# Six of eight units merged on TensorE, the scatter begun in the rank stage, preparation reordered, shorter stages by token

## The reference, cut to what matters

```python
x = x + conv(ln_c(x))                          # x: (4, 64, 64, 256), layer norm over channels
t = tokens(x)                                  # 16384 tokens of 256
t = t + ffn(ln_t(t), W_gat, att_src, att_dst, b_gat, ln_gamma, ln_beta, W1, b1, W2, b2, edge_index)

def conv(x):                                   # per image: 4096 tokens
    corr = einsum('bmf,bnf->bmn', x3, x3) / F
    s = -sort(-corr, axis=-1)                  # each row of 4096 sorted, descending
    return take(s, ranks, axis=-1)             # 256 ranks, evenly spaced from 1 to 4095

def ffn(x, ...):                               # a graph attention (1048576 edges) routes 4 experts
    h = x @ W_gat; e = leaky_relu(a_src[src] + a_dst[dst])
    ee = exp(e - segment_max(e, dst)[dst]); alpha = ee / segment_sum(ee, dst)[dst]
    scores = layernorm(segment_sum(h[src] * alpha, dst) + b_gat).mean(heads)
    w = softmax(top_2(scores))
    return sum over experts of gate * (gelu(x @ W1[e] + b1[e]) @ W2[e] + b2[e])
```

## Time and profile before

| | us |
|---|---|
| median of 3 runs | 30719.29 (30713.63 to 30737.62) |
| the profiled execution's own time | 30707.68 |
| its span | 30706.0 |

### The profile page before, as it was taken

One profiled execution on the slowest core, in us unless ns is written; L12 is line 12 of the kernel. 1 busy time (PEld: TensorE's weight loads), 2 busy tenths in 40 slices (PEclk: granted clock), 3 DMA queues, 4 the chain that ended last, 5 costly groups with the idle time before them and its releaser, 6 DMA issues. The chain is left out here.

```text
span 30706.0 us, 514061 instructions
## 1 busy us (share of the span) xinstructions
PE 26132.4 (85%) x182003; PEld 12435.8 (40%) x182004; DVE 27866.9 (91%) x31378; ACT 20334.5 (66%) x30319; POOL 19826.0 (65%) x9076
## 2 busy tenths in 40 slices
PE   3888889989999999999999999989999999982473
PEld 2555543333333333333333333333333333332473
DVE  6888858999999999999999999999999999996435
ACT  1777777767767767767776776767777777763720
POOL 0000007898888888888888888888888898402610
PEclk8999999999999999999999999999999999996655
DMA  2000000000000000000000000000000000000104
GB/s 93 2 2 2 2 19 4 7 7 7 7 7 7 12 7 7 7 7 7 7 12 7 7 7 7 7 6 7 13 7 7 7 6 7 7 5 13 15 11 136
DMA packets 651242, 393.57 MB, mean 13 GB/s; under 512 B 425132, under 2 KB 604336, under 8 KB 646448
## 3 DMA queue, kind: packets, MB, share of 16 engines
q1 hardware_dynamic: 338034, 311.42, 3.2%
q0 software_dynamic: 290304, 22.40, 1.1%
q10 hardware_dynamic: 20288, 25.70, 0.2%
HBM read 196.49 MB, written 162.34 MB: 12 GB/s over the span
## 5 line engine op out<-in xcount | busy, mean ns | idle before, releaser
L1584 POOL DMA_INDIRECT sorted_d<-word_s,place_s x8192 | 18974.3, 2316 | 2642.8 <-issue 2476.8
L1496 ACT ACTIVATE z<-psum 128x1024 f32<-128x1024 f32 x10089 | 10181.7, 1054 | 2004.0 <-PE psum L1223 1258.5
L1395 DVE TENSOR_TENSOR arena<-arena 128x1024 f32<-128x1024 f32 (+16 forms) x5760 | 10843.3, 1883 | 442.8 <-ACT arena L1492 397.0
L1396 DVE TENSOR_TENSOR arena<-arena 128x1024 f32<-128x1024 f32 (+16 forms) x5760 | 10837.1, 1881 | 0.0
L1223 PE MATMUL psum<-z,net 64*64 64x512 f32 x72504 | 9163.8, 601 | 140.3 <-ACT z L1496 111.2
L1496 ACT ACTIVATE cst<-psum 128x1024 f32<-128x1024 f32 x5015 | 5303.4, 1058 | 979.2 <-PE psum L1223 635.0
L1223 PE MATMUL psum<-cst,net 64*64 64x512 f32 x36040 | 4826.4, 602 | 77.9 <-ACT cst L1496 51.0
L1223 PEld LDWEIGHTS psum<-z,net 64*64 64x64 f32 x72504 | 2425.6, 131 | 5275.3 <-issue 5178.5
L1216 PE MATMUL psum<-rows,arena 128*128 128x256 f32 x8192 | 2017.6, 402 | 1629.4 <-ACT arena L1492 1597.1
L1578 POOL DMA_DIRECT2D word_s<-words_d x64 | 37.5, 586 | 4830.5 <-ACT cst L1496 4702.1
L1038 ACT ACTIVATE arena<-cst,arena 128x128 bf16<-128x128 f32 x8320 | 2632.8, 389 | 610.1 <-PE psum L966 513.4
(11 more groups left out here) (231 smaller groups left out, 23519.1 us busy)
## 6 DMA issues: line engine op xcount, KB each, us to landing
sorted_d<-word_s,place_s POOLq DMA_INDIRECT x8192
y_d<-ys SPq DMA_DIRECT2D x256, 256.0 KB
arena<-y_d SPq DMA_DIRECT2D x64, 1024.0 KB, 5.5
arena<-in_x SPq DMA_DIRECT2D x34, 512.0 KB, 5.1
x<-in_x SPq DMA_DIRECT2D x65, 256.0 KB
xnt_d<-arena SPq DMA_DIRECT2D x32, 512.0 KB, 3.1
hk_d<-arena SPq DMA_DIRECT2D x32, 512.0 KB, 4.3
arena<-hk_d SPq DMA_DIRECT2D x4, 4096.0 KB
```

The source lines that it names most:

```text
L1395: nc.vector.tensor_tensor(hi_out, hi_in, lo_in, ALU.max)
L1396: return nc.vector.tensor_tensor(lo_out, hi_in, lo_in, ALU.min)
L1496: last = nc.scalar.activation(flat, bank, ACT.Abs)
L1584: pool.indirect_dma_start(out=b.sorted_d[:, :], out_offset=bass.IndirectOffsetOnAxis(ap=place_s[:, s, j:j + 1], axis=0), in_=word_s[:, s, ...
```

## The change

- Six of the eight units are merged. VectorE's stages with p = 128 have 1024 keys per row, and TensorE has 272 ticks to a pair.
- The `carry` copies are ScalarE's, at fixed half ticks of the order (`CARRY_AT`: 2, 3, 19, 26, 78, 84, 142, 149, 214, 220 of 272). VectorE still waits for them (`carried`).
- In `prepare` the token part comes first, with statistics a step ahead, two buffers towards TensorE and ScalarE, and the next load issued before the stores. The edge part follows, and TensorE and ScalarE run the whole front end of pair 0 (`FIRST_PAIR`) between its groups of count matmuls. SP stores the words.
- In `rank` the places are turned to integers and stored super by super, and POOL scatters the first 14 supers. The other 50 follow in `pool_rows`, each group of 8 DMAs waiting for a count of VectorE's finished half stages. The one-hots lie elsewhere in the arena; their number and size are the same.
- In `segment_max` 4 of the 16 spreading operations are VectorE's.
- In `segment_sum` one-hots are bf16, values and look-up rows are split into three bf16 parts (24 and 60 columns instead of 8 and 20), the small operations are done once for four chunks, and the words are loaded a round ahead.

```diff
+EARLY_SUPERS = 14
+PACE = 8
...
-MERGED_UNITS = 4
+MERGED_UNITS = 6
...
+    ALONE = 10
...
             with sp.Fori(0, N_X) as i:
...
+                    k = i * 2 + s
+                    sp.wait_ge(normed, k + 1)
+                    nxt = ((k + 2) % (TILES // 4))
+                    sp.dma_start(xs[s], x_q[bass.ds(nxt, 1)].rearrange("o p q d -> (o p) q d")).then_inc(x_in[s], 16)
+
+                    sp.wait_ge(turned_copied, k + 1)
+                    tok = k * 512
                     sp.dma_start(b.xnt_d[:, :, bass.ds(tok, 512)], xt[s]).then_inc(xt_out[s], 16)
                     sp.dma_start(b.hk_d[:, :, bass.ds(tok, 512)], ht[s]).then_inc(xt_out[s], 16)
-
-                    nxt = ((i * 2 + s + 2) % (TILES // 4))
-                    sp.dma_start(xs[s], x_q[bass.ds(nxt, 1)].rearrange("o p q d -> (o p) q d")).then_inc(x_in[s], 16)
+            for s in range(2):
+                sp.wait_ge(xt_out[s], 32 * N_X)
+            sp.dma_start(b.xnt[:], b.hk_d[:, :, 0:M]).then_inc(b.hk_in, 16)
+            sp.dma_start(b.rows[:], b.xnt_d[:, :, 0:2 * P]).then_inc(b.rows_in, 16)
+            for k in range(2 * N_E):
+                sp.wait_ge(words_made, k + 1)
+                sp.dma_start(b.words_d[:, k * ECHUNK:(k + 1) * ECHUNK], words[:, k % 2, :]).then_inc(word_out[k % 2], 16)
+                if k + 2 < 2 * N_E:
+                    sp.wait_ge(edges_read, k + 1)
+                    load_edges(k + 2)
...
+            with dve.Fori(0, N_X) as i:
+                for s in range(2):
+                    k = i * 2 + s
+                    t = Tally(dve, dve_step, base=k * X_STEPS + (x_base + 2))
+                    statistics(t, 1 - s, i + (1 + s))
+                    dve.wait_ge(std_ready, k + 1)
+                    newton(nc, t, rstd, rtmp, var[:, s, :], std[:, s, :])
+
+                    dve.wait_ge(turned, i * 2)
+                    for q in range(4):
+                        last = nc.vector.tensor_scalar(xn[s][:, q, :], xs[s][:, q, :], mv[:, s, q, 0:1],
+                                                       rstd[:, q:q + 1], ALU.subtract, ALU.mult)
+                    last.then_inc(normed, 1)
...
-                    pe.wait_ge(turned_copied, k)
+                    pe.wait_ge(turned_copied, i * 2)
...
+            pe.wait_ge(turned_copied, 2 * N_X)
+            done = 0
+            for k in range(2 * N_E):
+
+                pe.wait_ge(edges_read, k)
+                for u in range(SUBS):
+                    pe.wait_ge(hot_ready, k * SUBS + u + 1)
+                    l16 = hot16[u % 2].rearrange("p j b -> p (j b)")
+                    l8 = hot8[u % 2].rearrange("p j b -> p (j b)")
+                    for g in range(8):
+                        last = nc.tensor.matmul(psum[:, 6, 0:64], l16[:, g * 128:g * 128 + 128],
+                                                l8[:, g * 64:g * 64 + 64], start=(u == 0 and g == 0),
+                                                stop=(u == SUBS - 1 and g == 7))
+                    last.then_inc(hot_used, 1)
+                    upto = max(k * SUBS + u + 1 - ALONE, 0) * len(FIRST_PAIR) // (2 * N_E * SUBS - ALONE)
+                    for s, n in FIRST_PAIR[done:upto]:
+                        front_matmuls(nc, b, pe, z, 0, s, n)
+                    done = upto
 
...
+                    deviation(1 - s, k + 2)
...
+            for s, n in FIRST_PAIR:
+                front_copy(nc, b, act, z, 0, s, n)
...
+                    dve.wait_ge(rank_used, (k + 1) * GROUPS)
+                    v = places[:, s, :]
+                    nc.vector.tensor_scalar(over[:, s, :], v, BIG, 2.0 * BIG, ALU.is_lt, ALU.mult).then_inc(over_made, 1)
+                    dve.wait_ge(over_made, k + 1)
+                    dve.wait_ge(place_out[s], i * 16)
+                    nc.vector.scalar_tensor_tensor(place_i[:, s, :], v, -BIG, over[:, s, :], ALU.add,
+                                                   ALU.add).then_inc(place_made, 1)
...
+            with sp.Fori(0, SUPERS // 2) as i:
+                for s in range(2):
+                    k = i * 2 + s
+                    sp.wait_ge(place_made, k + 1)
+                    sp.dma_start(b.place_d[:, bass.ds(k * SUPER, SUPER)], place_i[:, s, :]).then_inc(place_out[s], 16)
...
+            with pool.Fori(0, EARLY_SUPERS // 2) as i:
+                for s in range(2):
+                    pool.wait_ge(place_out[s], (i + 1) * 16)
+                    scatter(nc, b, pool, i, s)
+            for k in range(SCAT_SEMS):
+                pool.wait_ge(b.scattered[k], EARLY_SUPERS * SCAT // SCAT_SEMS * 16)
...
+def scatter(nc, b, pool, i, s, paced=False):
+
+    per_sem = SCAT // SCAT_SEMS
+    pool_in, scattered = b.pool_in, b.scattered
+    for k in range(SCAT_SEMS):
+        pool.wait_ge(scattered[k], i * (2 * per_sem * 16) + (s * per_sem * 16 if s else 0))
+    pool.sem_inc(b.settled[1], 1)
+    col = (i * 2 + s) * SCAT
+    pool.dma_start(b.word_s[:, s, :], b.words_d[:, bass.ds(col, SCAT)]).then_inc(pool_in[s], 16)
+    pool.dma_start(b.place_s[:, s, :], b.place_d[:, bass.ds(col, SCAT)]).then_inc(pool_in[s], 16)
+    pool.wait_ge(pool_in[s], (i + 1) * 32)
+    pool.sem_inc(b.settled[1], 1)
+    for j in range(SCAT):
+
+        if paced and j % PACE == 0:
+            pool.wait_ge(b.sorted_, ((i - EARLY_SUPERS // 2) * 2 + s) * 2 * N_FULL + (j * 2 * N_FULL // SCAT + 1))
+            pool.sem_inc(b.settled[1], 1)
+        pool.indirect_dma_start(
+            out=b.sorted_d[:, :], out_offset=bass.IndirectOffsetOnAxis(ap=b.place_s[:, s, j:j + 1], axis=0),
+            in_=b.word_s[:, s, j:j + 1], in_offset=None, bounds_check=CAPACITY - 1,
+            oob_is_err=False).then_inc(scattered[j % SCAT_SEMS], 16)
 
 
...
+    work = [(1 if s >= FIRST_MERGE else (M - LO) / M) if s < N_FULL else 0.5 for s in range(N_STAGES)]
+    CARRY_AT = {(p, which): round(H_BODY / BODY_PAIRS * sum(work[:first_of(p) + which + 1]) / sum(work))
+                for p in MERGES for which in range(2)}
...
-            def carry(source, target, to, p, which, i, s):
-
-                dve.wait_ge(sorted_, (i * N_FULL + (s + 1)) * 2)
-                nc.vector.tensor_copy(edges_of(target[:, 0:to], p, which),
-                                      edges_of(source[:, 0:to], p, which)).then_inc(carried, 1)
...
-                        for which in range(2):
-                            if h == 0 and k == p >> (which + 1):
-                                f = first_of(p)
-                                carry(keys[f % 2], keys[(f + 1) % 2], whole, p, which, i, f)
...
+            def carry(i, p, which):
+
+                s = first_of(p)
+                act.wait_ge(sorted_, (i * N_FULL + (s + 1)) * 2)
+                to = 2 * (M - LO) if s < FIRST_MERGE else 2 * M
+                nc.scalar.activation(edges_of(keys[(s + 1) % 2][:, 0:to], p, which),
+                                     edges_of(keys[s % 2][:, 0:to], p, which), ACT.Copy).then_inc(carried, 1)
+
+            def carries(i, place):
+                for (p, which), at in CARRY_AT.items():
+                    if place == at:
+                        carry(i, p, which)
 
...
+                        sorts = (body - back) * BODY_PAIRS + (r - 1)
+                        if not isinstance(body, int) or 0 <= sorts < PAIRS - 1:
+                            carries(sorts, place)
...
+            for place in range(H_BODY // BODY_PAIRS):
+                ffn_piece(PAIRS - 2, place)
+                carries(PAIRS - 1, place)
...
+            with pool.Fori(EARLY_SUPERS // 2, ECOLS // SCAT // 2) as i:
...
+                    scatter(nc, b, pool, i, s, paced=True)
...
+            def spread_share(i, s):
+
+                dve.wait_ge(got_in[s], (i + 1) * (16 * EQ))
+                dve.wait_ge(other_ready, i * N + (s + 1))
+                dve.sem_inc(b.settled[0], 1)
+                for h in range(HEADS):
+                    for q in DVE_Q:
+                        last = nc.vector.tensor_scalar(spread[s][:, h, q, :], other[s][:, q, :], MASKED,
+                                                       got[s][:, q, h:h + 1], ALU.mult, ALU.add)
+                last.then_inc(share_ready[s], 1)
...
+                for s in (0, 1):
+                    spread_share(i, s)
...
+                    if s + 2 < N:
+                        spread_share(i, s + 2)
...
-                        for q in range(EQ):
+                        for q in ACT_Q:
...
+                    pe.wait_ge(share_ready[s], i + 1)
...
+                sp.wait_ge(low_ready, i)
+                sp.dma_start(word.rearrange("p (s q) -> p s q", s=N), round_of(sorted_c, i)).then_inc(word_in, 16)
+                sp.wait_ge(value_ready, i)
+                sp.dma_start(got.rearrange("p (s q) f -> p s (q f)", s=N), round_of(gathered_c, i)).then_inc(got_in, 16)
...
+                dve.wait_ge(word_in, (i + 1) * 16)
+                nc.vector.tensor_scalar(low, word, 255, None, ALU.bitwise_and).then_inc(low_ready, 1)
```

(29 more changed lines are left out.)

492 lines of the change are left out of this document (235 added, 257 removed).

## The result

The changed kernel takes 37,704 us (median of 4 runs, 37,617 to 37,728), the kernel before 30,719 us (4 runs, 30,714 to 30,738). The ratio is 1.2267, 95% interval 1.2246 to 1.2289. I had forecast 29,947 us and at most 30,650.

A forecast was written before the change was run, and what follows sets the result against it. VectorE was taken to bound the sort, 27 us a pair ahead of TensorE, which would become the bound. 30706 + 52 + 260 - 618 (sort) - 100 - 367 = 29933, + 14 = 29,947 us; range 29,350 to 30,650.

The forecast's parts named there:

- Rank: Rank stage: +45 us for added VectorE operations and drains, +215 for the scatter beside it; +260 in the sum.
- what a DMA of POOL does to VectorE: Rank: each of 1792 scatter DMAs slows VectorE by 0.12 us, +215 us; bounds 0 and 450.
- Rival (b): Rank: POOL's scatter DMAs outlast the stage, at 2.62 us each 980 us more, whole 30,927 us; chance 0.12.
- My estimate from it, 6220 us for rank: Rank: by the skill's two-port lock a DMA takes 3.4 us, rank 6220 us, whole about 32,330 us.
- The carries: Sort: ScalarE's ten edge copies a pair add 4.7 us exposed; bounds 0, or all 11.5 and 3.4 more.
- Rival (c): Sort: edge copies fully exposed, VectorE and ScalarE waiting for each other, pair 370 to 372.5 us, whole 30,570 to 30,720; chance 0.15.
- TensorE's side (355.3): Sort: with two more merged units TensorE needs 355.3 us a pair and becomes the bound, 14 us above VectorE.
- VectorE's (341): Sort: VectorE's pair falls from 364.3 to 341 us, by 15.2 for halved stages and 8.1 for edge copies, +0.2.
- VectorE's lead over TensorE of 27 us: Sort, kernel before: VectorE leads TensorE by 27 us of 364 a pair; that margin decides the case.
- segment_max: segment_max: moving four of ScalarE's 16 spreading operations to VectorE saves 100 us; at most -230, at least +60.
- segment_sum: segment_sum: bf16 one-pass matmuls and fewer small operations cut a round to 12.2 us, -367 us; bounds -200 and -450.
- Prepare: Prepare: token part 224 us instead of 331, edge part 512, stage 761 us, +52; bounds -60 and +120.

The follow-up runs named there:

- e1: Changed kernel with no scatter in rank, all 64 supers scattered paced in the sort stage: 35,662 us, rank 3451 us.
- f2: Changed kernel without scatter in rank, carries on VectorE, POOL's pacing removed: 29,790 us, on a chip where the kernel before takes 30,436.
- f3: Changed kernel without scatter in rank or pacing, carries on VectorE, 24 register moves on POOL after each DMA: 29,808 us (kernel before 30,436).
- f4: Changed kernel, no rank scatter or pacing, carries on VectorE, 24 register moves per DMA, four merged units for six: 29,922 us (kernel before 30,436).
- h1: Changed kernel, no rank scatter or pacing, carries on VectorE, four merged units, segment_max spreading all on ScalarE: 31,142 us, ratio 1.0175 to kernel before.
- i1: Changed kernel, no rank scatter or pacing, carries on VectorE, four merged units, spreading on ScalarE, scatter begun after pair 1's front end: 30,623 us, ratio 0.9973.
- i2: Changed kernel, no rank scatter or pacing, carries on VectorE, six merged units, spreading on ScalarE, scatter begun after pair 1's front end: 37,684 us.
- f1: Changed kernel with no scatter in rank and carries on VectorE, pacing kept: 29,805 us, on a chip where the kernel before takes 30,436.
- g3: Changed kernel without scatter in rank, carries on VectorE, no pacing: 38,784 us, on a chip where the kernel before takes 30,734.
- sets 1 to 5: Five groups of follow-up runs, each on one chip beside the kernel before, which took 30,717, 30,436, 30,734, 30,718 and 30,707 us.

## Why the prediction was wrong, point by point

**Rank (+260 forecast, +2188 measured).** The step that failed is "what a DMA of POOL does to VectorE", priced at 0.12 us from the slowing of a small operation. In rank the one-hots take 286 to 289 ns beside the scatter against 280 without: 0.01 us. What the DMA does is make TensorE's and ScalarE's updates late, 1.31 us a DMA (e1). The work without the scatter is 157 us shorter than before, where I had added 45: VectorE's reduces wait 151 us, not 291. Rival (b) named the right stage and sign by the wrong way. POOL was never the bound: its DMAs ran every 1.28 us, half of the 2.50 us from which (b) decides, and ended at 3985, 2649 us before the stage did. By the Trainium skill, "SBUF — State Buffer", The "DVE blocks DMA" trap, an operation of VectorE in a two-port mode keeps GpSimd from writing a DMA's descriptors. My estimate from it, 6220 us for rank, is near the measured 5795, and still it does not explain them: here a DMA takes 974 ns, so the two-port lock does not show beside these one-hots. In the sort, beside rows of tensor_tensor, a DMA takes 1.83 us in the median (f2) and up to 146. It is held up there, though beside another operation than the copy that the trap names, and by less than the page's 3100 ns in the median. (My limit for POOL in rank, 2.07 us a DMA, comes to 2.11 by the terms that stand there; at 1.28 measured it changes nothing.)

**The carries (4.7 us a pair forecast, 27 measured: 388.7 less 361.5).** This is the second step that failed. I had both waits in hand (ScalarE at place 19, VectorE at place 214) and let the first cost nothing and the second "just fit". Such a wait, at a fixed place in a queue on which a second engine's pace depends, cost in both directions: 23 us on one side and 28 on the other. Rival (c) had the mechanism and, with 370 to 372.5, over half of the size.

**TensorE's side (355.3) and VectorE's (341).** VectorE's is right: three pairs of the changed kernel hold 1014.5 us of its work, 338 a pair. That TensorE sets the pair without the other two effects is right too, but at 361.5 to 362.4 us, 6 to 7 over the term, and no run tells where these come from. So the two units are worth 1.7 us a pair (f3 and f4) and not the 8.8 that lie between 364.1 and the term: TensorE and VectorE are now both full, and the merging has little left to give.

**What I did not see: the margin was doing a job.** I wrote that VectorE's lead over TensorE of 27 us decides the case. It does, the other way round: VectorE without a gap is what keeps POOL's DMAs 2.1 us apart. Take the lead away and every gap of VectorE lets POOL run at 1.28 us; that makes TensorE late, which makes VectorE's gap longer. h1's second window shows one such round, and i1 against i2 what it costs. Of the +4611 us of the sort, 1550 are the longer pair (24.6 x 63), 3440 the scatter beside 49 pairs (458.9 less 388.7), and -380 the two ends.

**A sign of it lay in the trace of before.** In segment_max 752 gathers are issued 1.30 us apart, and VectorE's reduce waited there for nobody, with 98 of TensorE's updates late by 1142 us in all, and none in f1: this row of the kernel before, and the same group in f1 on the other chip.

```profile
L1700 DVE TENSOR_REDUCE arena<-psum 128x4 f32<-128x2048 f32 x188 | 430.9, 2292 | 656.2 <-remote 608.7 <-issue 44.6 <-PE psum L1738 2.9
```

```profile
L1782 DVE TENSOR_REDUCE arena<-psum 128x4 f32<-128x2048 f32 x188 | 430.0, 2287 | 237.4 <-PE psum L1823 222.0 <-issue 14.9
```

**segment_max (-100 forecast, +155 measured).** Back on ScalarE alone the spreading gives 1280 us again (h1, i1), as before. So VectorE's share costs 150 us where updates are late: TensorE waits 614 us of the stage for it (L1791), for it stands in VectorE's queue behind reduces that wait for late updates. I had priced it at four operations of 0.25 us, exposed in a third of the chunks. Where they are not the stage takes 1029 us with the share; without it I have no run there.

**segment_sum (-367 forecast, -172 measured).** Outside my bounds. Two operations of successive rounds:

```profile
36811.71 2.50 DVE L1988 TENSOR_TENSOR arena<-cst,arena 128x512 bf16<-128x512 f32 x4
...
36827.74 2.50 DVE L1988 TENSOR_TENSOR arena<-cst,arena 128x512 bf16<-128x512 f32 x4
```

A round takes 16.0 us, not 12.2. TensorE's share fell even further than I said (212 / 47 = 4.5 us), but I had taken a round as the sum of TensorE's work and small change. It is one chain through three engines, in which TensorE, ScalarE and VectorE take turns; that batching the rounds' four chunks made it stricter I did not test.

**Prepare (+52 forecast, +125 measured).** Just outside my bound of +120. The edge part is as worked out, 517 us for 512. The token part is not: VectorE begins the one-hots at 321.4 us, not 249, so double buffering took 35 us off it and not 107. The step takes 9.2 us, not 7.0. What I left out of it is the load: in 31 of the 32 steps VectorE's statistics wait for it, half of the time from 28 to 321 us. That this wait sets the step no run has tried.

```profile
DVE arena L791 <- DMA arena<-in_x: 145.7, 31, 5.7
```

## What to carry to other kernels

Before taking work off the engine that leads, ask what its fullness holds back: a queue that it throttles by accident will run free once it has gaps. Give such a queue a brake of its own, at a rate that a run has shown to be harmless (here 2.3 us between DMAs, or one in flight), and budget it, since a brake that is too strong makes the queue the bound. Read "remote" in a profile as a question, above all when DMAs are being issued in a row, and repeat a surprising result on a second chip before building on it.

## What the runs showed of the hardware

- Indirect DMAs issued by POOL every 1.28 us delayed the semaphore updates of TensorE, ScalarE and VectorE by up to some 60 us, on four of the five chips of sets 1 to 5; at 2.29 and 2.93 us they hardly did (TensorE's in the sort: 308 and 81 us in all, against 12,088). Rates between 1.28 and 2.1 us were not tried by themselves, nor the rate apart from the number in flight.
- The number of words did not matter: 16 partitions for 128 left rank at 5830 us (5794), with 32 packets to a DMA in both.
- One and the same kernel takes 38,784 us on one chip and 29,790 on another (g3 and f2), where the kernel before differs by 1%. What differs in the chips stays open.
- An indirect DMA of 128 words takes 0.97 us on POOL beside bf16 tensor_scalars and 1.83 us in the median beside rows of f32 tensor_tensors (f2); with one in flight the next began 2.0 us after the last had left POOL (2.93 us from start to start).
